# Expert tiles: gathered rows turned by a transposing DMA instead of by TensorE

## The reference

```python
x = x + xattn(layernorm(x), ctx, Wq, bq, Wk, bk)
h = layernorm(x).reshape(4096, 1024)
logits = h @ gate_w.T + gate_b                      # 32 experts
topk_logits, topk_idx = top_k(logits, 4); w = softmax(topk_logits)
# for each of the 4 experts of a row:
gate = minimum(h @ w_gate[e] + b_gate[e], 7)        # 1024 -> 512
up   = clip(h @ w_up[e] + b_up[e], -7, 7)
out  = ((up + 1) * gate * sigmoid(1.702 * gate)) @ w_down[e] + b_down[e]
x = x + sum over the 4 of w * out
```

## Time and profile before

| what | value |
|---|---|
| median of 3 runs | 3280.85 us (3279.0 to 3282.75) |
| the profiled execution | 3284.01 us |
| its span, first to last instruction | 3282.2 us |
| mean granted TensorE clock | 0.973 |
| TensorE busy | 3120.8 us, 95% |
| VectorE, ScalarE, GpSimd busy | 52%, 39%, 18% |

### The profile page before, as it was taken

How to read it: one execution, slowest core, us unless ns; L and a number is a source line. 1 busy time by engine, 2 the same in 40 slices (tenths; PEclk the granted TensorE clock), 3 DMA queues, 4 the chain that set the end, 5 groups by cost and what they waited for, 6 DMA issues and landing times.

```text
span 3282.2 us, 46620 instructions
## 1 busy us (share of the span) xinstructions
PE 3120.8 (95%) x15456; PEld 1609.9 (49%) x15457; DVE 1720.9 (52%) x2851; ACT 1280.6 (39%) x1299; POOL 595.1 (18%) x502
## 2 busy tenths in 40 slices
PE   6799899995999999999999999999999999999997
PEld 3455555553455444455455444544555445455553
DVE  4576767774453544554544545444455444454432
ACT  3553434422342434443433434344344333343421
POOL 0023323322111111111111111111111111111111
PEclk8899999997999999999999999999999999999999
DMA  4123222354564555556555655655565655555432
GB/s 149 64 104 124 103 84 104 104 166 146 144 171 117 148 154 154 174 159 198 155 155 150 173 154 166 192 173 144 142 171 164 197 156 153 154 163 144 110 63 58
DMA packets 210439, 468.03 MB, mean 143 GB/s; under 512 B 57761, under 2 KB 57761, under 8 KB 210114
## 3 DMA queue, kind: packets, MB, share of 16 engines
q1 hardware_dynamic: 164514, 314.84, 27.2%
q0 software_dynamic: 45856, 152.33, 22.2%
HBM read 354.64 MB, written 112.46 MB: 142 GB/s over the span
## 4 chain that ended last, share of the span: by engine, by line
PE 71%; DMA 3%; SPq 1%; issue 1%; ACT 0%; DVE 0%; POOL 0%; ACTq 0%; POOLq 0%; DVEq 0%
PE psG L1167 22%; PE psU L1167 22%; PE psY L1189 22%; PE psX L1173 4%; PE psA L1180 2%; DMA bias<-in_L_ffn_b_down 2%; DMA idxg<-slots 0%; SPq L959 0%; DMA idxs<-slots 0%; SPq L112 0%; DMA acc<-y,idxs 0%; SPq L962 0%; DMA xg<-xn_tab,idxg 0%; ACT aT L1057 0%; DVE gt L1122 0%
## 5 line engine op out<-in xcount | busy, mean ns | idle before, releaser
L1189 PE MATMUL psY<-W,aT 128*128 128x512 f16 x3456 | 777.9, 382 | 23.1 <-ACT aT L1057 23.1
L1167 PE MATMUL psG<-W,xT 128*128 128x512 f16 x3456 | 772.4, 380 | 2.9 <-ACT xT L1053 2.9
L1167 PE MATMUL psU<-W,xT 128*128 128x512 f16 x3456 | 769.4, 379 | 0.0
L1167 PEld LDWEIGHTS psG<-W,xT 128*128 128x128 f16 x3456 | 338.8, 98 | 413.0 <-issue 6.1
L1189 PEld LDWEIGHTS psY<-W,aT 128*128 128x128 f16 x3456 | 339.7, 98 | 406.2 <-ACT aT L1057 24.5
L1167 PEld LDWEIGHTS psU<-W,xT 128*128 128x128 f16 x3456 | 338.2, 98 | 375.6
L1114 DVE SCALAR_TENSOR_TENSOR y<-bias,idxs,y 128x1024 f32<-128x1024 f32 x144 | 185.0, 1284 | 544.7 <-ACT y L1064 544.7
L123 DVE SCALAR_TENSOR_TENSOR W<-stage,W 128x2048 f16<-128x2048 f32 x192 | 438.7, 2285 | 4.8 <-ACT W L118 4.8
L1021 POOL DMA_INDIRECT acc<-y,idxs x144 | 227.4, 1579 | 1011.9 <-DVE y L1114 996.3
L1064 ACT ACTIVATE y<-psY,idxs 128x1024 f32<-128x1024 f32 x144 | 160.5, 1114 | 604.6 <-DMA idxs<-slots 577.9
L118 ACT ACTIVATE W<-stage 128x2048 f16<-128x2048 f32 x192 | 365.1, 1902 | 10.8 <-issue 5.5
(11 more groups left out here) (136 smaller groups left out, 2305.1 us busy)
## 6 DMA issues: line engine op xcount, KB each, us to landing
stage<-in_L_ffn_w_gate SPq DMA_DIRECT2D x64, 1024.0 KB
stage<-in_L_ffn_w_up SPq DMA_DIRECT2D x64, 1024.0 KB
stage<-in_L_ffn_w_down SPq DMA_DIRECT2D x64, 1024.0 KB
stage<-in_x SPq DMA_DIRECT2D x32, 512.0 KB
xr<-in_x SPq DMA_DIRECT2D x32, 512.0 KB
acc<-xr SPq DMA_DIRECT2D x32, 512.0 KB
xn_tab<-x2h SPq DMA_DIRECT2D x32, 512.0 KB
bias<-in_L_ffn_b_down SPq DMA_DIRECT2D x32, 512.0 KB, 13.6
```

Source lines behind the costliest of these rows:

```text
L1167: op = pe.matmul(ps[:], xT[:, k, :, a], weights(par, c, offset + k * I, I), start=k == 0 and n == 0, stop=k == KH - 1 and n == 2)
L1189: op = pe.matmul(psY[:, h * HALF:(h + 1) * HALF], aT[:, k, :, a], weights(par, c, 2 * KH * I + k * H + h * HALF, HALF), start=k == 0 and n ...
```

## The change

TensorE's transposes of the gathered rows, their PSUM tile `psX` and their semaphore go. After the rows of a tile have landed in `xg`, SyncE issues one `dma_start_transpose` from `xg` to a new SBUF tile `xT_next`, and ScalarE copies `xT_next` to `xT` once the up matmuls of the tile before are done. So that two-byte elements can be turned in blocks, `x2h` and with it a row of `xn_tab` now hold all low halves first and then all high halves, and `xT` has its 16 blocks in that order. SyncE waits for ScalarE's copy before each transpose; GpSimd waits for the transpose's end before the next gather. `LOAD` changes from chunks 3, 4 / 5 / 6, 7, 8 to 2, 3 / 4, 5 / 6, 7, and the first stage loads one chunk fewer ahead.

```diff
--- before.py
+++ after.py
@@ -151,7 +151,7 @@
         xnh = sb("xnh", [P, H, 2], F16)
         ah = sb("ah", [P, 2, L, 2], F16)
         xs2 = sb("xs2", [P, H], F32)
-        x2h = sb("x2h", [P, 2, H, 2], F16)
+        x2h = sb("x2h", [P, 2, 2, H], F16)
         x2T = sb("x2T", [P, KH, P], F32)
         before = sb("before", [P, P], F32)
         upto = sb("upto", [E, E], F32)
@@ -407,12 +407,12 @@
                     sp.dma_start(acc_rows[bass.ds(n, 1)].rearrange("o p h -> (o p) h"), xr[:, s % 2, :]).then_inc(s_x2out[s % 2], 16)
                     sp.wait_ge(s_lo2, tile(b2, s + 1))
                     sp.dma_start(xn_rows[bass.ds(n, 1)].rearrange("o p h -> (o p) h"),
-                                 x2h[:, s % 2].rearrange("p h a -> p (h a)")).then_inc(s_xnout[s % 2], 16)
+                                 x2h[:, s % 2].rearrange("p a h -> p (a h)")).then_inc(s_xnout[s % 2], 16)
 
                     if s < NT - 2 or b1 is not None:
                         alone(sp, s_x2out[s % 2], per(8 * NT, b2, 16 * (s // 2 + 1)), s_past)
                         load_x(xr, s_xr, batch(b2 if s < NT - 2 else following(b2)), (s + 2) % NT)
-                    if b1 is None:
+                    if b1 is None and s < NT - 1:
                         sp.wait_ge(s_wlo, s - 1)
                         g["load_chunk"](sp, 0, s - 2 + RING)
 
@@ -531,7 +531,7 @@
 
                     act.wait_ge(s_xnout[n % 2], per(8 * NT, bt, 16 * (n // 2 + 1)))
                     act.wait_ge(s_xs2, tile(bt, n + 1))
-                    act.activation(x2h[:, n % 2, :, HI], xs2[:], ACT.Copy, scale=S_ROWS).then_inc(s_hi2, 1)
+                    act.activation(x2h[:, n % 2, HI, :], xs2[:], ACT.Copy, scale=S_ROWS).then_inc(s_hi2, 1)
                 if b1 is not None:
                     guarded(act, own, hi_parts)
                     if s >= 1 and b2 is None:
@@ -783,7 +783,7 @@
                 if late:
                     bt, n = late
                     dve.wait_ge(s_hi2, tile(bt, n + 1))
-                    dve.scalar_tensor_tensor(out=x2h[:, n % 2, :, LO], in0=xs2[:], scalar=S_ROWS, in1=x2h[:, n % 2, :, HI],
+                    dve.scalar_tensor_tensor(out=x2h[:, n % 2, LO, :], in0=xs2[:], scalar=S_ROWS, in1=x2h[:, n % 2, HI, :],
                                              op0=ALU.mult, op1=ALU.subtract).then_inc(s_lo2, 1)
                 if latest:
 
@@ -888,7 +888,7 @@
 
 
     CUT = [[0, 1], [2, 3], [4, 5]]
-    LOAD = [[3, 4], [5], [6, 7, 8]]
+    LOAD = [[2, 3], [4, 5], [6, 7]]
     assert NCHUNK == 6 and len(CUT) == MIN_TILES
 
     with ExitStack() as ctx:
@@ -905,7 +905,8 @@
         idxg = sb("idxg", [P, 4], I32)
         idxs = sb("idxs", [P, 4], I32)
         xg = sb("xg", [P, 2 * H], F16)
-        xT = sb("xT", [P, KH, P, 2], F16)
+        xT = sb("xT", [P, 2 * KH, P], F16)
+        xT_next = sb("xT_next", [P, 2 * KH, P], F16)
         gt = sb("gt", [P, I], F32)
         sg = sb("sg", [P, I], F32)
         up = sb("up", [P, I], F32)
@@ -913,11 +914,9 @@
         ahl = sb("ahl", [P, I, 2], F16)
         aT = sb("aT", [P, KI, P, 2], F16)
         y = sb("y", [P, H], F32)
-        xg_w = xg[:, :].bitcast(F32)
         ahl_w = ahl[:, :, :].rearrange("p i a -> p (i a)").bitcast(F32)
         psG = psum("psG", [P, HALF], F32)
         psU = psum("psU", [P, HALF], F32)
-        psX = psum("psX", [P, KH * P], F32)
         psA = psum("psA", [P, KI * P], F32)
         psY = psum("psY", [P, 2 * HALF], F32)
 
@@ -930,7 +929,7 @@
         s_added = sem("tile_added")
         s_G = sem("gate_done")
         s_U = sem("up_done")
-        s_X = sem("x_transposed")
+        s_xtr = sem("x_transposed")
         s_A = sem("act_transposed")
         s_Y = sem("down_done")
         s_gread = sem("gate_read")
@@ -964,14 +963,20 @@
 
         @block.sync
         def _(sp):
+            def transpose_rows(i):
+
+                alone(sp, s_xg, 16 * i + 16, s_past)
+                sp.dma_start_transpose(out=xT_next[:, :, :], in_=xg[:, :]).then_inc(s_xtr, 16)
+
             load_slots(sp, idxg, 0, s_idxg)
             load_bias(sp, 0, 0)
-            sp.wait_ge(s_xg, 16)
+            transpose_rows(0)
             load_slots(sp, idxg, 1, s_idxg)
 
             def step(i, e, j, more, prev_guard):
 
-                sp.wait_ge(s_xg, 16 * i + 32)
+                alone(sp, s_xTev, i + 1, s_past)
+                transpose_rows(i + 1)
                 load_slots(sp, idxg, i + 2, s_idxg)
 
                 def prev():
@@ -1026,15 +1031,12 @@
             tt = start_of(pool, E)
             last = last_tile(pool)
             gather(0)
-            pool.wait_ge(s_X, 1)
-            gather(1)
-            pool.wait_ge(s_X, 2)
-            gather(2)
-            pool.wait_ge(s_X, 3)
-            gather(3)
+            for i in range(1, 4):
+                pool.wait_ge(s_xtr, 16 * i)
+                gather(i)
             scatter(0)
             with pool.Fori(1, last) as j:
-                pool.wait_ge(s_X, j + 3)
+                pool.wait_ge(s_xtr, 16 * j + 48)
                 gather(j + 3)
 
                 pool.wait_ge(s_scat, 16 * j)
@@ -1048,9 +1050,10 @@
 
         @block.scalar
         def _(act):
-            def evac_x(i):
-                act.wait_ge(s_X, i + 1)
-                act.activation(xT[:].rearrange("p k q a -> p (k q a)").bitcast(F32), psX[:], ACT.Copy).then_inc(s_xTev, 1)
+            def take_rows(i):
+                act.wait_ge(s_xtr, 16 * i + 16)
+                act.activation(xT[:].rearrange("p k q -> p (k q)").bitcast(F32),
+                               xT_next[:].rearrange("p k q -> p (k q)").bitcast(F32), ACT.Copy).then_inc(s_xTev, 1)
 
             def evac_a(i):
                 act.wait_ge(s_A, i + 1)
@@ -1064,7 +1067,7 @@
                 act.activation(y[:], psY[:], ACT.Copy, scale=idxs[:, 2:3].bitcast(F32)).then_inc(s_y0, 1)
 
             act.sem_inc(s_y0, 1)
-            evac_x(0)
+            take_rows(0)
 
             def step(i, e, par, t0, j, more, prev_guard):
                 def free_gate_up():
@@ -1087,7 +1090,8 @@
                 guarded(act, prev_guard, lambda: evac_a(i - 1))
                 if j is not None:
                     guarded(act, more, lambda: cut_one(1))
-                evac_x(i + 1)
+                alone(act, s_U, i + 1, s_past)
+                take_rows(i + 1)
                 act.wait_ge(s_act, i + 1)
                 act.activation(ahl[:, :, HI], av[:], ACT.Copy, scale=S_ACT).then_inc(s_ahi, 1)
                 guarded(act, prev_guard, lambda: weigh_y(i - 1))
@@ -1164,14 +1168,9 @@
             def rows_times(ps, par, offset, done):
                 for k in range(KH):
                     for n, (a, c) in enumerate(PASSES):
-                        op = pe.matmul(ps[:], xT[:, k, :, a], weights(par, c, offset + k * I, I),
+                        op = pe.matmul(ps[:], xT[:, a * KH + k, :], weights(par, c, offset + k * I, I),
                                        start=k == 0 and n == 0, stop=k == KH - 1 and n == 2)
                 op.then_inc(done, 1)
-
-            def transpose_rows():
-                for n in range(KH):
-                    op = pe.transpose(psX[:, n * P:(n + 1) * P], xg_w[:, n * P:(n + 1) * P], ident[:])
-                op.then_inc(s_X, 1)
 
             def transpose_act(i):
                 pe.wait_ge(s_ahi, i + 1)
@@ -1207,13 +1206,9 @@
                 guarded(pe, prev_guard, between)
                 weights_cut(2 * PER_W)
                 rows_times(psU, par, KH * I, s_U)
-                pe.wait_ge(s_xg, 16 * i + 32)
-                transpose_rows()
                 guarded(pe, prev_guard, lambda: down(i - 1, 1 - par if first else par))
                 weights_cut(3 * PER_W)
 
-            pe.wait_ge(s_xg, 16)
-            transpose_rows()
             with pe.Fori(0, PAIRS) as pair:
                 for par in range(2):
                     e = pair * 2 + par
```

## The result

The changed kernel is slower: a median of 3341.61 us against 3280.43, ratio 1.0154 with the interval [1.0083, 1.0225]. The median counts all four executions, the ratio leaves out the longest of them (3380.78 us), a slow one. Measured once more beside the experiments the kernel gave 3330.47 against 3282.02, ratio 1.0158 [1.0121, 1.0196]. The forecast was 3156 us, faster with a chance of 0.57, so the time moved the other way; it lies inside the stated range only because that range reached into the rival of the other side. The profiled execution took 3310.3 us with a span of 3308.5 and is the quickest of the four, which spread over 2%.

A forecast was written before the change was run, and what follows sets the result against it. TensorE alone was taken to set the expert stage's period. From 3284.0 us, less 125.3 for transposes and 2 for the attention stage, plus 2.9 at the start, less 3.2 to the median, gave 3156 us; range 3135 to 3700.

The forecast's parts named there:

- the rival of the other side: Expert stage: a slow transpose makes the transpose-gather loop the period; some 3530 us, up to 3780; chance 0.35.
- What bounds the kernel: Expert stage: TensorE alone sets the period, 16.85 us a tile with no gap.
- What goes: Expert stage: eight transposes a tile leave TensorE, 144 x 0.87 = 125.3 us off the path; new period 15.98 us.
- The copy on ScalarE: Expert stage: copying the transposed rows takes 0.95 to 1.2 us with four microseconds to spare; cost 0.
- The transposing DMA: Expert stage: the unknown, a 512 KB transposing transfer within SBUF, taken to fill the queue 1.9 to 4 us.
- T: Time the transposing DMA fills the queue beyond a small transfer's fixed part; taken at 1.9 to 4 us.
- Does it fit?: Expert stage: transposes, gathers and weights take 4.5 T + 50.4 us an expert against 71.9 of matmuls; fits below T 4.8.
- The weight loads: Expert stage: the list in twos keeps SP free but prefetches later; cost 0, at most 1 to 2 us a tile.
- The attention stage: x2h written in two contiguous halves gains 0 to 13 us; 2 us taken.
- Start: First rows: a DMA in place of TensorE's transposes costs +0.5 to +3.0 us, taken at +2.9.
- the slow transpose: Expert stage: T above 5.6 us makes transpose and gather the period, TensorE waits; some 3530 us, chance 0.35.
- Late chunks: Expert stage: the transpose fits but ScalarE's cuts wait for weights; some 3220 us, chance 0.08.

The follow-up runs named there:

- y1: The changed kernel with SyncE's index load of tile i+2 issued ahead of the transpose of tile i+1; 3240.76 us, ratio 0.9874 to the kernel before.
- y2: The changed kernel with a tile's chunk loads issued right behind transpose and index load, list 1, 2 / 3, 4 / 5, 6; 3144.29 us.
- x4: The changed kernel with each expert-stage chunk load moving an eighth of its bytes, later experts using stale weights; 3112.32 us, ratio 0.9486 to the kernel before.
- x2: The kernel before, transposes on TensorE, with only the new weight list 2, 3 / 4, 5 / 6, 7; 3253.54 us, ratio 0.9918 to the kernel before.
- x1: The changed kernel with the old weight list 3, 4 / 5 / 6, 7, 8; 3267.03 us, ratio 0.9960 to the kernel before.
- x3: The kernel before with only x2h written in contiguous halves, the expert stage then pairing wrong halves; 3268.68 us, ratio 0.9963 to the kernel before.
- y4: The changed kernel with the transposes issued by ScalarE on its own queue and SyncE freed to load the index row first; 3206.04 us, ratio 0.9763.

## Why the prediction was wrong

- *What bounds the kernel* and *What goes*: right. The period without loads is 15.97 us, forecast 15.98.
- *The copy on ScalarE*: right. 1.057 us within 0.95 to 1.2, and where the rows had landed in time it delayed no gate but the second, which has no down matmuls before it (1.32 us at 796.83).
- *The transposing DMA*: T was taken at 1.9 to 4 us and measured 2.75 alone, 4.0 as a mean share. The prediction feared T above all, and T was right. The piece is 256 bytes. Of the two estimates by the Trainium skill, the 21 us for sixteen blocks one after the other ("VectorE: DVE Perf Modes", The three transpose paths) doesn't hold here; the 1.5 us by the speed of a regular DMA ("Advanced Engine Details and Errata", X-Bar Transpose) is too short by a factor of 1.8.
- *Does it fit?* is the step that failed. It said: "It fits for T below 4.8 us". With T = 2.75 its formula gives 4 x 10.25 + 3 x 4.3 + 3.8 = 57.7 us for an expert of four tiles, under the 63.9 of its matmuls. The measured loop, from the transpose at 1512.22 to its counterpart at 1582.32, is 70.1 us. Tile by tile the formula has 14.5, 14.5 and, with the biases, 18.3 us, and 10.2 for the tile without loads; measured were 21.62, 16.75, 19.15 and 12.58.
  - The links were right, their lengths in a full queue were not. Most of it is the transpose's landing. Even alone it takes 4.3 us, 1.6 beyond T; with these, T + 4.3 + 1.6 = 8.7 us was the formula's price behind a pair of chunks and 12.5 with the biases, and 16.1, 10.4 and 13.7 us were measured.
  - The 4.3 us took the pair to be issued 1.6 us behind the gather, as in the kernel before. Here it is issued 1.36 us ahead of the transpose (1510.86 and 1512.22), nearly as the prediction's own *weight loads* had it (chunks at +12.2, the copy at +12.1). That makes 2 x 3.8 - 1.4 = 6.2 us a pair, and the formula still fits, with 63.4 us.
  - The rest had no term at all: the slow second half of such a landing, beside the scatter, and the hold of SyncE in the issue, up to 12 us, which keeps the index row back. The row's 2.5 us were read from a nearly idle queue and were 7.94 and 3.11 here.
  - y1 shows what the row's place behind the transpose costs (90 to 101 us); y2 and x4 show the part of the chunks ahead (186 to 197 and 218 to 229 us). The parts overlap, so they don't add up.
  - The mean over an expert also hid that a tile with two chunks or the biases must fit by itself: TensorE loses time there and can't win it back in the tiles that fit.
- *The weight loads*: costed at 0, with the prefetch as the danger. Alone they gained 27 us (x2); with the transposes they cost 63 to 75 (x1). ScalarE's waits for chunks cost nothing in x2. That the list puts two chunks ahead of each transpose was in the formula, with the wrong price.
- *The attention stage*: 2 us taken and 12 measured (x3), near the upper bound of 13.
- *Start*: +2.9 taken, +3.2 measured, just above its upper bound of +3.0.
- *Rivals*: the slow transpose ended on the right side for the wrong reason. Its condition was T above 5.6 us; alone the transpose took half of that. That the sign came with a chance of 0.37 is luck as far as the mechanism goes. *Late chunks* was no loss by itself.
- A term that was missing: after a wait TensorE can run at the lower clock for a while, 40.7 us on 138 us of waits.

## What to carry to other kernels

When work moves from an engine onto a DMA queue, price it with what stands ahead of it in that queue at that moment, not with its length alone: the same transposes cost 77 us behind the weight loads and gave 113 us in front of them. Ask, too, which other transfer will be under way when it comes late. Write the loop of buffers and waits as links, take each link's length from a row in which the queue is as full as it will be, and check the fullest tile rather than the mean. Of two loads, issue first the one that a chain waits for and last the one that has a period to spare.

## What the runs showed of the hardware

- A transposing DMA of 128 x 2048 two-byte elements within SBUF goes out as 2048 packets of 256 bytes, keeps the engines busy for at most 2.75 us alone (195 to 220 GB/s, kernel after), and lands 4.3 us after issue at the least.
- Behind two 1 MB loads and beside a scatter it can be much slower: in 1520.25 to 1527.75 us of the kernel after both together moved at 7 to 257 GB/s, and the transpose landed 16.1 us after its issue. The reason is open.
- Its issue holds the issuing engine: 1.5 us at the least, 5.7 in the median of all and 12.3 at most in the kernel after, where the issue of a plain 1 MB load takes 0.38 us.
- Issued on ScalarE's queue it is held too while chunks move on SyncE's: 7.60 us at 1514.58 in y4, 8.27 at most, with a median of 1.9.
- TensorE's granted clock was 0.51 for about 5 us behind a wait of 6.40 us, and 1.00 after that.
